# A recommendation kernel on one core: a ninth table looked up by matrix product in three of eight halves, gathers in groups of 4, 3, 4, 4, 3

## The chip, the cores and the metric

The kernel runs on one core of a Trainium2 chip. The metric is the device time of one execution in microseconds (us); lower is better. TensorE (PE) multiplies matrices, VectorE (DVE) and ScalarE (ACT) copy and compute, GpSimd (POOL) issues the gathers, SyncE (SP) issues most other DMA transfers. Each engine works through its own queue in order; they tell each other of progress by semaphores.

## The reference

```
e = stack([tbl_f[ids[:, f]] for f in range(26)], axis=1)     # (2048, 26, 128) fp32
combined = concatenate([e, dense_x[:, None, :]], axis=1)     # (2048, 27, 128)
interact = einsum('bfd,bgd->bfg', combined, combined)        # 27x27 dot products of each sample
z = interact[:, triu_i, triu_j]                              # the 351 pairs above the diagonal
h = concatenate([z, dense_x], axis=1)                        # (2048, 479)
h = relu(h @ W_top1 + b_top1)                                # 512
h = relu(h @ W_top2 + b_top2)                                # 256
y = h @ W_top3                                               # 1
```

There are 2048 samples and 26 embedding tables: eight of 1000 rows, nine of 1250, eight of 12500 and one of 125000.

## The kernel before, in words

The samples go through in 16 tiles of 128; two tiles make a half of 256 (h = t // 2), so there are 8 halves, an even and an odd tile each.

**Gathered tables.** 18 tables are fetched row by row: for each tile and table POOL issues one indirect DMA (L266) of 128 rows into one of 14 buffers of `rows`. PE turns each with a transpose (L283, `turn(t, n)`) into a bank of `ps_feat`, and ACT copies the bank into `feat` (L531). Gathers and turns go in five groups a tile, n = 0 to 4, of 4, 4, 4, 4 and 2 tables. Before a group POOL waits for `turned`, until the group that last used its buffers, 14 gathers earlier, was turned (`turns_before`, L93). For every tile this works out so: group 0 waits for group 1 of the tile before, group 1 for its group 2, group 2 for its group 3; groups 3 and 4 both wait for group 0 of their own tile.

**Kept tables.** The eight tables of 1000 rows lie in SBUF, each as 8 chunks of 125 rows, split into a high and a low part. They are looked up with products for a whole half, two tables at a time (`look_up(h, p)`, pairs p = 0 to 3). First PE spreads the ids of a pair over all partitions (L293, `spread_ids`) and ACT copies them to one of 3 buffers `ids_all` (L568). DVE compares them with row numbers and so builds one-hot columns (L766, `build`), in units of two chunks, in a ring of 10 units `hot`. PE multiplies each chunk twice (L319 high part, L321 low part), 32 matmuls a pair, and tells of each unit with `hot_free`. ACT copies the found rows (L544 for the even tile into `feat`, L547 for the odd one into `stage`, from where `unstage`, L574, moves them).

**Products and layers.** `products(t, b)`, b = 0 to 3, computes the dot products of a tile (L340, 16 matmul records each) into one of two banks `ps_gram`; ACT and DVE copy half each into `z` (L517, `take`). SP packs `z` into columns with nine small DMAs a tile (L205, `pack`). `split_half` (ACT, L586) and `rest_zp` (DVE, L752) split them, then come `layer1` and `layer2` (L349), `layer3` (L426).

**The order** of each engine is written out by hand for an even and an odd tile (`even(t)`, `odd(t)` on PE, ACT and DVE). The work that goes through the two `ps_feat` banks has one common numbering, `feat_turns` (L62); PE waits before using a bank until the use two places earlier was copied out (`bank_free`). On PE an even tile ends with `look_up(h, 3)`, `turn(t, 3)`, `layer2(h - 2, 0)`, `turn(t, 4)`, `layer2(h - 2, 1)`. The ids of the kept tables for the next half are loaded by SP (L214) and turned into numbers by ACT (L558, `number_ids`) into a second buffer.

## Time and profile before

| what | value |
|---|---|
| median of 3 runs | 522.01 us |
| lowest and highest | 517.69 and 525.85 us |
| the profiled execution | 515.37 us |
| its span, first to last instruction | 513.3 us |
| PE, DVE, ACT, POOL busy | 81, 48, 45, 55 % |
| mean granted TensorE clock | 0.900 |
| gathers | 288, mean 973 ns on POOL |

The span is what the profile covers; 2.07 us of the profiled execution lie around it. In a timeline each row is an instruction or a run of equal ones: start, duration, instruction with output and inputs and its count, and in brackets the idle time of that engine before it and who ended it. "issue" means that no wait was found; "remote" that the semaphore's update came at a time at which none of the instructions that send it had just ended. The ends of matmuls are modelled.

### The profile page before, as it was taken

The page shows a single profiled execution, that of the slowest core. Times are in us where ns is not written, and L with a number is a line of the kernel's source. Part 1 is how long each engine was busy: PE and PEld are TensorE (multiplying, and loading weights), DVE is VectorE, ACT ScalarE, POOL GpSimd, SP SyncE. Part 2 cuts the span into 40 slices and gives each one's busy share as a digit, 9 for nine tenths or more (in the row PEclk, how much of TensorE's full clock was granted, in tenths as well). Part 3 has the DMA queues.
Part 4 walks back from the last instruction along what each step waited for, and adds up shares of the span by engine and source line. Part 5 has one row for each costly group of instructions (what it writes and reads, how often), then busy time and mean ns, then how long its engine had stood idle before and what let it go on. Part 6 is the DMA issues. An engine that isn't in the chain of part 4 may idle for free.

```text
span 513.3 us, 8017 instructions
## 1 busy us (share of the span) xinstructions
PE 414.9 (81%) x2976; PEld 385.6 (75%) x2976; DVE 247.9 (48%) x715; ACT 232.7 (45%) x428; POOL 282.9 (55%) x297
## 2 busy tenths in 40 slices
PE   6697739586896979788797979889687877968887
PEld 4586638485895968787797859879687867967786
DVE  7383937434665245542564327533455426721332
ACT  3364516254453635434544435446354346334734
POOL 6666754656464663666546565466536575464210
PEclk9897959798897979999797988989798998997999
DMA  8921221122211121122211222121211222122100
GB/s 225 289 70 36 70 56 27 49 50 69 50 37 46 48 73 38 42 62 67 52 33 47 52 67 58 32 53 52 72 32 47 58 72 53 33 54 54 31 18 6
DMA packets 21488, 30.54 MB, mean 59 GB/s; under 512 B 6986, under 2 KB 15680, under 8 KB 21323
## 3 DMA queue, kind: packets, MB, share of 16 engines
q0 software_dynamic: 9312, 19.00, 14.3%
q1 hardware_dynamic: 11852, 10.83, 8.1%
q8 instruction: 24, 0.39, 0.3%
q10 hardware_dynamic: 287, 0.21, 0.2%
q14 instruction: 13, 0.11, 0.1%
HBM read 26.86 MB, written 0.01 MB: 52 GB/s over the span
## 4 chain that ended last, share of the span: by engine, by line
PE 46%; another core or an unknown queue 27%; ACT 19%; issue 7%; DMA 0%; ACTq 0%; DVE 0%
PE ps_gram L340 16%; PE ps_mlp L349 8%; PE ps_feat L319 7%; PE ps_feat L321 6%; ACT feat L531 5%; ACT z L517 3%; PE ps_feat L283 3%; ACT feat L574 3%; ACT feat L544 2%; PE ps_feat L316 2%; ACT ids_all L568 1%; PE ps_feat L293 1%; ACT stage L547 1%; PE ps_mlp L426 1%
## 5 line engine op out<-in xcount | busy, mean ns | idle before, releaser
L266 POOL DMA_INDIRECT rows<-in_tbl,ids_now x288 | 280.3, 973 | 197.5 <-PE ps_feat L283 76.1
L766 DVE TENSOR_SCALAR hot<-ids_all,row_no 125x256 fp32r<-125x256 f32 x512 | 159.0, 378 | 46.6 <-remote 21.2
L319 PE MATMUL ps_feat<-hot,table_hi 125*128 125x256 f32 x480 | 137.0, 316 | 17.6 <-issue 11.3
L321 PE MATMUL ps_feat<-hot,table_lo 125*128 125x256 f32 x480 | 135.0, 312 | 10.7 <-issue 10.6
L340 PE MATMUL ps_gram<-feat 128*123 128x108 f32 x1024 | 127.1, 281 | 3.8 <-ACT feat L531 3.7
L340 PEld LDWEIGHTS ps_gram<-feat 128*123 128x123 f32 x1024 | 121.9, 196 | 7.6 <-ACT feat L531 4.4
L517 DVE COPY z<-ps_gram 27x208 f32<-27x208 f32 x128 | 46.9, 367 | 156.6 <-PE ps_gram L340 87.0
L319 PEld LDWEIGHTS ps_feat<-hot,table_hi 125*128 125x128 f32 x480 | 105.0, 219 | 19.2 <-issue 10.3
L321 PEld LDWEIGHTS ps_feat<-hot,table_lo 125*128 125x128 f32 x480 | 104.9, 219 | 17.2 <-issue 16.9
L544 ACT COPY feat<-ps_feat 128x256 f32<-128x256 f32 x32 | 19.4, 607 | 143.7 <-remote 94.3
L517 ACT COPY z<-ps_gram 27x208 f32<-27x208 f32 x128 | 41.6, 325 | 94.9 <-remote 48.0
L531 ACT COPY feat<-ps_feat 128x512 f32<-128x512 f32 (+1 forms) x80 | 77.6, 976 | 10.7 <-remote 9.8
L283 PE MATMUL ps_feat<-ident,rows 128*128 128x128 f32 x288 | 46.5, 281 | 10.1 <-ACT stage L547 6.1
L293 PE MATMUL ps_feat<-ids_few_no,ident_r 128*128 128x512 f32 x32 | 17.8, 574 | 38.4 <-ACT stage L547 26.1
L283 PEld LDWEIGHTS ps_feat<-ident,rows 128*128 128x128 f32 x288 | 34.1, 146 | 13.4 <-issue 12.8
L293 PEld LDWEIGHTS ps_feat<-ids_few_no,ident_r 128*128 128x128 f32 x32 | 7.2, 228 | 42.7 <-ACT stage L547 19.0
L349 PE MATMUL ps_mlp<-zp_hi,w_hi 128*128 128x256 f32 x112 | 34.1, 304 | 1.9 <-ACT hid_lo_before L605 1.8
L349 PE MATMUL ps_mlp<-zp_lo,w_hi 128*128 128x256 f32 x112 | 32.7, 292 | 0.1
L349 PE MATMUL ps_mlp<-zp_hi,w_lo 128*128 128x256 f32 x112 | 32.5, 290 | 0.0
L752 DVE TENSOR_TENSOR hid_lo<-hid_lo_before,hid_hi 128x256 fp32r<-128x256 f32 x32 | 13.5, 422 | 26.8 <-ACT hid_hi L608 26.6
L349 PEld LDWEIGHTS ps_mlp<-zp_hi,w_hi 128*128 128x128 f32 x112 | 22.6, 202 | 2.4 <-ACT hid_lo_before L605 2.2
L349 PEld LDWEIGHTS ps_mlp<-zp_lo,w_hi 128*128 128x128 f32 x112 | 22.5, 201 | 0.6 <-issue 0.3
(73 smaller groups left out, 329.2 us busy)
## 6 DMA issues: line engine op xcount, KB each, us to landing
rows<-in_tbl,ids_now POOLq DMA_INDIRECT x288
table_lo_before<-in_tbl SPq DMA_DIRECT2D x8, 448.0 KB
dense<-in_dense_t SPq DMA_DIRECT2D x8, 128.0 KB
w_lo_before<-in_w SPq DMA_DIRECT2D x1, 1024.0 KB
zp_lo_before<-in_dense_t SPq DMA_DIRECT2D x8, 128.0 KB
zp_lo_before<-z SPq DMA_DIRECT2D x15, 39.0 KB
zp_lo_before<-z SPq DMA_DIRECT2D x15, 36.0 KB
w_lo_before<-in_w SPq DMA_DIRECT2D x1, 512.0 KB
```

The lines of the kernel that those rows point to most:

```text
L266: nc.gpsimd.indirect_dma_start(rows[:, row_at(t, f), :], None, gathered[f], bass.IndirectOffsetOnAxis(ap=ids_now[:, t, f:f + 1], axis=0),) ...
L283: mm = nc.tensor.transpose(ps_feat[at % 2][:, k * P:(k + 1) * P], rows[:, row_at(t, f), :], ident[:])
L293: nc.tensor.matmul(ps_feat[at % 2][:], ident_r[:, p:p + 1].broadcast_to([P, P]), ids_few_no[:].rearrange("p k s -> p (k s)"), start=True, ...
L319: nc.tensor.matmul(result, table_hi[:, CHUNK_AT[n] + ch, :], columns, start=first, stop=False)
L321: mm = nc.tensor.matmul(result, table_lo[:, CHUNK_AT[n] + ch, :], columns, start=False, stop=last)
L340: mm = nc.tensor.matmul(ps_gram[at % 2][0:FOUR, c, 0:4 * F], four[:, 0:FOUR], four.rearrange("d (j f) -> d j f", f=FPAD)[:, :, 0:F], start ...
L349: mm = nc.tensor.matmul(ps_mlp[at % 2][:, 0:HALF], w[:, c, n * P:(n + 1) * P], x[:, c, :], start=(c == 0 and k == 0), stop=(c == ZP_CHUNKS ...
L517: op = copy(z[q:q + F, :, 32 * j + BATCH * b:32 * j + BATCH * (b + 1)], ps_gram[at % 2][32 * j:32 * j + F, :, F * j + 1:F * (j + 1)].rearr ...
L531: copy(feature(t, group.start, group.stop), by_group(ps_feat[at % 2][:, 0:P * len(group)].rearrange("d (f s) -> d f s", s=P))).then_inc(em ...
L544: copy(feature(2 * h, GATHERED + first, GATHERED + stop), by_group(found[:, :, 0:P]))
L574: copy(feature(t, GATHERED, TABLES), by_group(stage[:])).then_inc(unstaged, 1)
L766: op = nc.vector.tensor_scalar(hot[0:VROWS, u % HOTS, c, :], ids[0:VROWS, k, :], row_no[0:VROWS, no + UNIT * i + c:no + UNIT * i + c + 1], ...
```

## The change

A ninth table, the first of 1250 rows (10 chunks of 125), is loaded into SBUF beside the eight. In halves 1, 2 and 4 (`LOOKED_UP_LAST`) it is looked up with products, as a fifth "pair" of one table (`LAST`); in the other five it is gathered, as before, as the last table of group 4. So a tile has 17 gathers in halves 1, 2 and 4 and 18 in the others, 282 in all for 288. The look-up stands on PE between `turn(t, 3)` and `layer2(h - 2, 0)` of the even tile; its ids are spread at the end of the odd tile before; DVE builds its one-hot columns before `take(t - 1, 3)`.

The groups are of 4, 3, 4, 4 and 3 tables (2 in the last one where the ninth is looked up). The buffers of `rows` go by a running count of gathers, and with them the waits: after a tile of 18 gathers group 0 of the next waits for group 2 (not 1) of the tile before; after one of 17 it waits for group 1, as it did. The waits of the other groups are as they were.

The numbers of the ids are written over the ids themselves (one buffer for the two, 32 partitions long), so SP loads the next half's ids only when all ids of this half are spread (before: once they were numbered). At the start the load of half 1's ids moves behind the weights, and the ninth table is loaded last; it is split on ACT and DVE behind the first odd tile. `y` has no buffer of its own: it is written over a row of `hid2`, and the wait for its transfer stands before the next `hid2` instead. The diff, cut:

```diff
@@ -23,22 +23,27 @@
 VROWS, SPRAYED = 125, 112
-CHUNKS = [8] * 8
+CHUNKS = [8] * 8 + [10]
 KEPT = len(CHUNKS)
+ALWAYS = KEPT - 1
+LOOKED_UP_LAST = (1, 2, 4)
 CHUNK_AT = [sum(CHUNKS[:n]) for n in range(KEPT + 1)]
 UNIT = 2
-UNITS = CHUNK_AT[KEPT] // UNIT
 HOTS = 10
 IDS = 3
-PAIRS = (KEPT + 1) // 2
-PAIR = [range(2 * p, min(2 * p + 2, KEPT)) for p in range(PAIRS)]
+
+IDS_ROWS = 32
+PAIRS = ALWAYS // 2
+LAST = PAIRS
+PAIR = [range(2 * p, min(2 * p + 2, KEPT)) for p in range(PAIRS + 1)]
 WHOLE_FIRST = 4
-SPLIT_AT = {n: i for i, n in enumerate([*range(WHOLE_FIRST, KEPT), *range(WHOLE_FIRST)])}
+SPLIT_AT = {n: i for i, n in enumerate([*range(WHOLE_FIRST, ALWAYS), *range(WHOLE_FIRST), ALWAYS])}
 SIZES = sorted(set(CHUNKS))
 ROW_NO_AT = {n: sum(SIZES[:i]) for i, n in enumerate(SIZES)}
-GATHERED = TABLES - KEPT
-GROUPS = [range(f, min(f + 4, GATHERED)) for f in range(0, GATHERED, 4)]
-TURNS = len(GROUPS)
+GATHERED = TABLES - ALWAYS
+GROUP_SIZES = (4, 3, 4, 4, 3)
+TURNS = len(GROUP_SIZES)
+GROUPS = [range(sum(GROUP_SIZES[:n]), sum(GROUP_SIZES[:n + 1])) for n in range(TURNS)]
 ROWS = 14
...
@@ -57,6 +62,20 @@
...
+def pairs_in(h):
+    return PAIRS + (h in LOOKED_UP_LAST)
+def group_of(t, n):
+    group = GROUPS[n]
+    return range(group.start, group.stop - (n == TURNS - 1 and t // 2 in LOOKED_UP_LAST))
+GATHERS = [(t, n, f) for t in range(TILES) for n in range(TURNS) for f in group_of(t, n)]
+GATHER_AT = {(t, f): i for i, (t, n, f) in enumerate(GATHERS)}
...
@@ -68,32 +87,42 @@
         h = t // 2
         if t % 2 == 0:
             order += [("tile", t, 0), ("pair", h, 2), ("tile", t, 1), ("ids", h + 1, 0), ("tile", t, 2),
-                      ("ids", h + 1, 1), ("pair", h, 3), ("tile", t, 3), ("tile", t, 4)]
+                      ("ids", h + 1, 1), ("pair", h, 3), ("tile", t, 3), ("pair", h, LAST), ("tile", t, 4)]
         elif h + 1 < HALVES:
             order += [("tile", t, 0), ("tile", t, 1), ("ids", h + 1, 2), ("tile", t, 2), ("pair", h + 1, 0),
-                      ("tile", t, 3), ("ids", h + 1, 3), ("pair", h + 1, 1), ("tile", t, 4)]
+                      ("tile", t, 3), ("ids", h + 1, 3), ("pair", h + 1, 1), ("tile", t, 4), ("ids", h + 1, LAST)]
         else:
             order += [("tile", t, n) for n in range(TURNS)]
-    return {x: n for n, x in enumerate(x for x in order if x[0] == "tile" or x[1] < HALVES)}
+    return {x: n for n, x in enumerate(x for x in order if x[0] == "tile" or x[1] < HALVES and x[2] < pairs_in(x[1]))}
 FEAT_AT = feat_turns()
+def ids_before(h):
+
+    return sum(pairs_in(i) for i in range(h))
+
+
 def units_before(h, n):
-    return UNITS * h + CHUNK_AT[n] // UNIT
+    return (sum(CHUNK_AT[PAIR[pairs_in(i) - 1].stop] for i in range(h)) + CHUNK_AT[n]) // UNIT
 def row_at(t, f):
-    return (GATHERED * t + f) % ROWS
+    return GATHER_AT[t, f] % ROWS
 def turns_before(t, f):
-    x = GATHERED * t + f - ROWS
-    return 0 if x < 0 else TURNS * (x // GATHERED) + x % GATHERED // 4 + 1
+    at = GATHER_AT[t, f] - ROWS
+    return 0 if at < 0 else TURNS * GATHERS[at][0] + GATHERS[at][1] + 1
+
+
+def landed(t, n):
+
+    return 16 * sum(len(group_of(i, n)) for i in range(t % 2, t + 1, 2))
 def bass_dlrm_tower(nc, dense_t, ids_gathered, ids_kept, gathered, kept, w1, b1, w2, b2, w3, out):
...
@@ -113,15 +142,16 @@
-        ident, ident_r = sb("ident", [P, P]), sb("ident_r", [P, PAIRS], F32R)
+        ident, ident_r = sb("ident", [P, P]), sb("ident_r", [P, PAIRS + 1], F32R)
         row_int, row_no = sb("row_int", [P, sum(SIZES)], I32), sb("row_no", [P, sum(SIZES)])
...
-        ids_few = sb("ids_few", [PAIRS, 2, HALF], I32)
-        ids_few_no = sb("ids_few_no", [P, 2, HALF], F32R)
+        at = (nc.sbuf_base + 31) // 32 * 32
+        ids_few_no = ctx.enter_context(nc.sbuf_tensor("ids_few_no", [P, 2, HALF], F32R, align_bytes=32))
+        ids_few = nc.alloc_sbuf_tensor_at("ids_few", [IDS_ROWS, 2, HALF], I32, offset=at)
         ids_all = sb("ids_all", [P, IDS, 2, HALF])
...
@@ -210,7 +245,7 @@
-                    sp.wait_ge(ids_few_ready, h)
+                    sp.wait_ge(ids_spread, ids_before(h))
                 sp.dma_start(ids_few[:], ids_kept[:, h * HALF:(h + 1) * HALF].rearrange("(p k) s -> p k s", k=2)
...
@@ -230,16 +265,17 @@
             load_ids(0)
-            for n in range(KEPT):
+            for n in range(ALWAYS):
                 load_table(sp, n)
             load_dense(0)
-            load_ids(1)
             sp.dma_start(w1_sb[:], w1).then_inc(weights_landed, 16)
...
             sp.dma_start(b2_sb[:], b2).then_inc(biases_landed, 16)
+            load_ids(1)
             load_dense(1)
+            load_table(sp, ALWAYS)
             for t in range(2, TILES + 2):
...
@@ -259,9 +295,10 @@
             for t in range(TILES):
-                for n, group in enumerate(GROUPS):
-                    if turns_before(t, group.stop - 1) > 0:
-                        pool.wait_ge(turned, turns_before(t, group.stop - 1))
+                for n in range(TURNS):
+                    group = group_of(t, n)
+                    if turns_before(t, group[-1]) > 0:
+                        pool.wait_ge(turned, turns_before(t, group[-1]))
                     for f in group:
...
@@ -441,6 +480,7 @@
                 turn(t, 3)
+                look_up(h, LAST)
                 layer2(h - 2, 0)
...
@@ -465,6 +505,7 @@
                 layer1(h - 1, 3)
+                spread_ids(h + 1, LAST)
...
@@ -527,51 +568,54 @@
...
-                if h > 0:
-                    act.wait_ge(ids_spread, PAIRS * h)
-                copy(ids_few_no[0:PAIRS, :, :], ids_few[:]).then_inc(ids_few_ready, 1)
+                copy(ids_few_no[0:IDS_ROWS, :, :], ids_few[:]).then_inc(ids_few_ready, 1)
...
@@ -716,6 +762,7 @@
             odd(1)
+            split_table(ALWAYS)
             act.wait_ge(weights_landed, 16 * 2)
...
@@ -799,6 +846,7 @@
                 put_dense(t)
+                build(h, LAST)
                 take(t - 1, 3)
```

The order of the gathers on POOL, from the last group of tile 0 on (in_tbl_N is the table, "waits turned" opens a group). Before:

```order
L266 DMA rows<-in_tbl_21,ids_now 128x128 [waits turned]
L266 DMA rows<-in_tbl_24,ids_now 128x128
L266 DMA rows<-in_tbl_0,ids_now 128x128 [waits turned]
L266 DMA rows<-in_tbl_1,ids_now 128x128
L266 DMA rows<-in_tbl_4,ids_now 128x128
L266 DMA rows<-in_tbl_5,ids_now 128x128
L266 DMA rows<-in_tbl_6,ids_now 128x128 [waits turned]
```

And after:

```order
L303 DMA rows<-in_tbl_21,ids_now 128x128 [waits turned]
L303 DMA rows<-in_tbl_24,ids_now 128x128
L303 DMA rows<-in_tbl_0,ids_now 128x128
L303 DMA rows<-in_tbl_1,ids_now 128x128 [waits turned]
L303 DMA rows<-in_tbl_4,ids_now 128x128
L303 DMA rows<-in_tbl_5,ids_now 128x128
L303 DMA rows<-in_tbl_6,ids_now 128x128
L303 DMA rows<-in_tbl_7,ids_now 128x128 [waits turned]
```

The last group has three gathers (21, 24 and 0, the ninth table), and the next tile begins one gather later.

DVE, from the last build of pair 3 in even tile 4 on (L766 and L813 build one-hot columns, L517 and L558 are takes, L775 and L822 put the dense feature). Before:

```order
L766 TENSOR_SCALAR hot<-ids_all,row_no 125x256 x16
L517 COPY z<-ps_gram 27x26x8 x2
L775 COPY feat<-dense 128x4x32
L517 COPY z<-ps_gram 27x26x8 x2
L766 TENSOR_SCALAR hot<-ids_all,row_no 125x256 x16
```

And after:

```order
L813 TENSOR_SCALAR hot<-ids_all,row_no 125x256 x16
L558 COPY z<-ps_gram 27x26x8 x2
L822 COPY feat<-dense 128x4x32
L813 TENSOR_SCALAR hot<-ids_all,row_no 125x256 x10
L558 COPY z<-ps_gram 27x26x8 x2
L813 TENSOR_SCALAR hot<-ids_all,row_no 125x256 x16
```

Ten comparisons stand ahead of the last take of the tile before.

PE, at the end of the same even tile: the last matmuls of pair 3, the turn of group 3, what follows. Before:

```order
L319 MATMUL ps_feat<-hot,table_hi 128x256
L321 MATMUL ps_feat<-hot,table_lo 128x256
L283 MATMUL ps_feat<-ident,rows 128x128 x4
L349 MATMUL ps_mlp<-hid_hi,w_hi 128x256
L349 MATMUL ps_mlp<-hid_lo,w_hi 128x256
```

And after:

```order
L358 MATMUL ps_feat<-hot,table_hi 128x256
L360 MATMUL ps_feat<-hot,table_lo 128x256
L320 MATMUL ps_feat<-ident,rows 128x128 x4
L358 MATMUL ps_feat<-hot,table_hi 128x256
L360 MATMUL ps_feat<-hot,table_lo 128x256
```

Behind the turn now stand 20 matmuls of the look-up, of which the first two are shown, and `layer2` comes after them.

## Rows read from the trace of the kernel before

**Rows 1.** The page: span, busy time by engine, chain that ended last.

```profile
span 513.3 us, 8017 instructions
PE 414.9 (81%) x2976; PEld 385.6 (75%) x2976; DVE 247.9 (48%) x715; ACT 232.7 (45%) x428; POOL 282.9 (55%) x297
PE 46%; another core or an unknown queue 27%; ACT 19%; issue 7%; DMA 0%; ACTq 0%; DVE 0%
```

**Rows 2.** Waits, longest first: engine, line waited for, us, times, longest us.

```profile
ACT feat L544 <- remote: 94.3, 18, 9.5
```

**Rows 3.** Timeline, POOL, tiles 9 to 11: start, us, instruction, idle before and releaser.

```profile
292.23 0.94 POOL L266 DMA_INDIRECT rows<-in_tbl,ids_now  x1 [1.17 <-PE ps_feat L283]
...
306.98 0.94 POOL L266 DMA_INDIRECT rows<-in_tbl,ids_now  x1 [2.46 <-remote]
...
324.46 0.94 POOL L266 DMA_INDIRECT rows<-in_tbl,ids_now  x1 [5.50 <-PE ps_feat L283]
...
333.36 0.94 POOL L266 DMA_INDIRECT rows<-in_tbl,ids_now  x1 [1.72 <-remote]
...
345.79 0.94 POOL L266 DMA_INDIRECT rows<-in_tbl,ids_now  x1 [2.64 <-remote]
```

**Rows 4.** Timeline, PE, the same stretch.

```profile
296.10 1.87 PE L340 MATMUL ps_gram<-feat 128*123 128x108 f32 x16
...
299.26 0.60 PE L283 MATMUL ps_feat<-ident,rows 128*128 128x128 f32 x4
...
321.80 1.95 PE L340 MATMUL ps_gram<-feat 128*123 128x108 f32 x16
...
325.67 0.36 PE L319 MATMUL ps_feat<-hot,table_hi 125*128 125x256 f32 x1
...
329.55 0.60 PE L283 MATMUL ps_feat<-ident,rows 128*128 128x128 f32 x4
...
334.94 0.63 PE L283 MATMUL ps_feat<-ident,rows 128*128 128x128 f32 x4 [0.45 <-ACT feat L531]
335.40 2.85 PE L340 MATMUL ps_gram<-feat 128*123 128x108 f32 x16
```

**Rows 5.** Timeline, ACT, the same stretch.

```profile
306.55 0.67 ACT L517 COPY z<-ps_gram 27x208 f32<-27x208 f32 x2 [6.54 <-remote]
...
323.79 0.66 ACT L517 COPY z<-ps_gram 27x208 f32<-27x208 f32 x2 [0.88 <-PE ps_gram L340]
...
333.07 0.59 ACT L544 COPY feat<-ps_feat 128x256 f32<-128x256 f32 x1 [5.83 <-remote]
...
338.29 0.66 ACT L517 COPY z<-ps_gram 27x208 f32<-27x208 f32 x2 [1.25 <-issue]
...
345.50 0.64 ACT L544 COPY feat<-ps_feat 128x256 f32<-128x256 f32 x1 [5.93 <-remote]
345.91 0.43 ACT L547 COPY stage<-ps_feat 128x256 f32<-128x256 f32 x1
```

**Rows 6.** Timeline, PE, end of even tile 10.

```profile
342.75 0.60 PE L283 MATMUL ps_feat<-ident,rows 128*128 128x128 f32 x4
...
346.49 0.41 PE L283 MATMUL ps_feat<-ident,rows 128*128 128x128 f32 x2
```

**Rows 7.** Groups by shape: busy us, mean ns of one, idle before.

```profile
L266 POOL DMA_INDIRECT rows<-in_tbl,ids_now x288 | 280.3, 973 | 197.5 <-PE ps_feat L283 76.1 <-issue 73.5 <-remote 46.1
L293 PE MATMUL ps_feat<-ids_few_no,ident_r 128*128 128x512 f32 x32 | 17.8, 574 | 38.4 <-ACT stage L547 26.1 <-ACT ids_all L568 4.9 <-ACT ids_few_no L558 3.9
L766 DVE TENSOR_SCALAR hot<-ids_all,row_no 125x256 fp32r<-125x256 f32 x512 | 159.0, 378 | 46.6 <-remote 21.2 <-PE ps_feat L321 14.9 <-PE ps_feat L316 5.2
L752 DVE TENSOR_TENSOR table_lo<-table_lo_before,table_hi 125x1024 fp32r<-125x1024 f32 x8 | 9.5, 1222 | 0.4 <-ACT table_hi L692 0.4
```

**Rows 8.** Timeline, SP's DMA issues, pack of tile 9.

```profile
339.11 7.42 SPq L205 DMA_DIRECT2D zp_lo_before<-z  x9
```

**Rows 9.** Timeline, ACT, tile 11.

```profile
354.74 1.05 ACT L586 CAST zp_hi<-zp_lo_before 128x1024 fp32r<-128x1024 f32 x1 [0.44 <-issue]
```

85 lines of the change are left out of this document (50 added, 35 removed).

## The prediction

> **What bounds the kernel now.** I read the page first. PE is the busiest engine, 414.9 of 513.3 us, yet it carries only 46 % of the chain that ended last; 27 % stands under "another core or an unknown queue" and 19 % under ACT [rows 1]. One core runs, so the 27 % must be waits whose release the profile can't place. The list of waits says where: ACT before L544 (it empties a looked-up pair) waited 94.3 us "remote", 18 times [rows 2]. So I went to the timelines of POOL, PE and ACT over tiles 9 to 11.
>
> The last product of tile 8 ends on PE at 296.10 + 1.87 = 297.97; ACT, which has nothing else to do, copies it at 306.55, after 6.54 us idle [rows 4, 5]. That is 8.6 us late. The product that ends at 321.80 + 1.95 = 323.75 is copied at 323.79, 0.04 us late [rows 4, 5]. What differs is POOL. Its gathers follow each other every 0.94 + 0.30 = 1.24 us. From 292.23 to 306.98 - 2.46 = 304.5 it issues ten in one run; in the 5.5 us before 324.46 it issues none [rows 3]. The same shows in the even tile: the look-up's last matmul ends just before 329.55, ACT sees it at 333.07, and POOL's run of six ends at 333.36 - 1.72 = 331.6 [rows 3 to 5]. Pair 3 is over before 342.75, ACT sees it at 345.50, POOL's run of eight ends at 345.79 - 2.64 = 343.15 [rows 3, 5, 6]. So an update by PE that falls late into a run of gathers is seen 1.4 to 2.4 us after the run's end. Early in a run it isn't late: the product that ends at 335.40 + 2.85 = 338.25, 4.9 us into a run, is copied at 338.29 [rows 3 to 5]. Rows never are late: the gathers that end at 292.23 - 1.17 = 291.06 are turned at 299.26 [rows 3, 4]. The half thus goes round a loop: run of gathers, PE's updates come through, `turned` lets POOL start the next run. Gathers cost time though PE never waits for a row.
>
> **The look-up's price on PE.** Pair 2 takes from 325.67 to 329.55, 3.88 us for 32 matmuls, 0.121 each [rows 4]. Twenty more are 2.42 us. Two transposes go (about 0.1 us each), and an ids matmul of 256 columns comes: half of 574 ns, 0.29 [rows 7]. Net 2.5 us in each of three halves, **+7.5**. All of it is on the chain, since PE is what runs there between two waits.
>
> **Its place.** The look-up needs the bank of pair 3, which ACT frees at 345.91 + 0.43 = 346.34 [rows 5]. Before, PE filled the time from 342.75 to 346.49 with a `layer2` and turned group 4 at 346.49 [rows 6]. Now it reaches the look-up first, stands until 346.34, and `layer2` (12 matmuls, 1.45 us) comes after it and has lost its cover. That happens in halves 2 and 4; half 1 has no `layer2` there yet. **+2.9.**
>
> **The split of the ninth table**: DVE 1.222 x 1.25 = 1.53 us [rows 7], and the cast on ACT ahead of it, for which I take as much, once, between tiles 1 and 2; other work of PE covers them partly: 0 to 3, I take **+1**.
>
> **Gathers saved.** Six, each 1.24 us of a run [rows 3]. In the even tile of halves 1, 2 and 4 the second run has seven for eight; in the odd tile the run behind the ten has three for four. Where updates wait for the run's end, each saved gather brings PE forward by 1.24: six are -7.5; if the lateness isn't the gathers' doing, 0. The rows speak for the first: **-7.5**.
>
> At this place a rule of the Trainium skill speaks against my reading. "SBUF — State Buffer", section "SBUF: two separate sides", says that DMA ports and engine ports are disjoint, that a DMA can't be slowed by compute nor the reverse, and that PE never waits on anyone there. By it the saved gathers would bring nothing. The trace doesn't show which port is busy; it shows the lateness next to the runs. The second rival below gives the time for that.
>
> **The groups.** In halves 1, 2, 4 the runs keep their shape (6, 7, 4 and 10, 3, 4). In halves 3, 5, 6, 7 group 0 waits for group 2 of the tile before, so an even tile has runs of 7, 7, 4 (before 6, 8, 4) and an odd one 7, 7, 4 (before 10, 4, 4). Even tile: the first run ends 1.24 later. The second started at 333.36 with group 1's turn; now it starts with group 2's, which ends at 334.94 + 0.63 = 335.57 [rows 3, 4], pushed by the same 1.24: 336.8 and 0.3 to start, 3.8 later. With one gather less it ends 2.6 later. If the look-up of pair 3 is caught by it, +2.6; but it now falls earlier into the run, where updates came through, and then pair 3 is seen at once, 1.2 earlier than at 345.50. Between +2.6 and -1.2, near the middle: +0.7, four times. Odd tile: the run of ten, behind which the product was 8.6 us late, becomes seven, 3.7 us shorter; the next is seven for four and gives back all of it or nothing: 0 to -4, I take -2, three times. Together 4 x 0.7 - 3 x 2 = **-3** (bounds -17 and +10.6).
>
> **Costed at nothing.** DVE's ten comparisons (378 ns each, 3.8 us [rows 7]) stand before the last take, and the later of them wait for pair 3's first units; the take, now at about 338.3 as ACT's [rows 5], may slip to where pair 3's updates come through, 345.5. PE needs it for the product after next. SP's `pack`, nine DMAs in 7.42 us from 339.11 [rows 8], then starts near 346 and ends at 353.6, and ACT splits at 354.74 [rows 9]: the cover of 8.2 us shrinks to 1 and what the landing takes may stick out; but the half is up to 4 us longer there too. If it fails it costs some 2 us, three times. The load of ids now waits for the last spread, in a half with the ninth table just before the product at 321.80 [rows 4]; the numbering waits for it, and what is queued behind the numbering on ACT, L544, comes only at 333.07 [rows 5]: 11 us of cover. The pack of the tile before, behind that load on SP, slips too, but is needed only at 354.74 [rows 9]. `y` in `hid2` is sent well before `hid2` is written again.
>
> **The sum.** 7.5 + 2.9 + 1 - 7.5 - 3 = +0.9 on the profiled execution's 515.37 us (513.3 us of it span). The median of the runs is 522.01, 6.6 above it, and I add to that: **523 us**.
>
> **The rivals.**
> *Shorter runs break the lateness.* If the 8.6 us come from a run's length and not from the sum of gathers, the odd tiles of halves 3, 5, 6 gain 4 each (-12), the even ones 1.2 each four times (-4.8), and the saved gathers 7.5: 11.4 - 7.5 - 12 - 4.8 = -13, 509 us. For it: six gathers made 3.4 us of lateness (329.7 to 333.07), ten 8.6 [rows 4, 5], more than in proportion. Against it: the second run follows at once, and the total of gathers in such a half stays 36.
> *The lateness is PE's own.* Runs may end late because `turned` comes late, not the reverse. Then neither shape nor number of gathers counts, and 7.5 + 2.9 + 1 = +11.4 remain: 533 us. By the rule that the Trainium skill's "SBUF — State Buffer", section "SBUF: two separate sides", states, it would come out so. Against it: PE is as busy before 323.75, without gathers, and on time.
> *The second run catches the look-up.* Slower: in the four even tiles the longer and later run holds pair 3, +2.6 each (10.6), the odd tiles gain nothing, and half of the saved gathers lie where PE would have waited anyway (-3.7): 11.4 + 10.6 - 3.7 = +18, 540 us. It decides from the point where the units of pair 3 fall more than some 5 us into the run; before, an update 4.9 us into one was on time [rows 3 to 5].
> *The ninth table isn't worth its place at all*, the ids late: ACT would stand before L558; 11 us of cover make this the least likely, +3 a half, 532.
>
> **How the numbers follow.** Forecast 0.48 (515 to 531), shorter runs 0.20, PE's own 0.17, second run 0.12, ids 0.03. The range for 8 in 10 reaches to most of the faster case and up to the slower one: 505 to 539. A measurement of this kernel tells 2 %, 10.4 us, from no change: faster is below 511.6, slower above 532.4. Faster: two thirds of 0.20 and a tail of the forecast, 0.18. Slower: half of 0.20, the 0.12 and a tail, 0.26. The rest, 0.56, is no change.
>
> **What would show it.** Right, if in tile 11's like the product before the run of seven is seen within 2.5 us of the run's end; if PE stands before the look-up of the ninth table until ACT's L547 counterpart ends; if tiles of halves 1, 2 and 4 are longer than their neighbours by 0 to 4 us. The gather term is wrong if a half with 34 gathers has as much "remote" waiting as one with 36. The forecast falls if the odd tiles of halves 3, 5, 6 shrink by more than 4 us, or if the even ones grow by more than 3; or if ACT waits before its split of `zp`.

## The result, and the profile after

The kernel after takes 540.72 us (median of 4 runs, 537.57 to 545.97) beside 521.36 us of the kernel before (4 runs, 517.69 to 525.85): ratio 1.0376, interval 1.0285 to 1.0466. It is slower; 523 with a range up to 539 and 0.26 for slower had been forecast. The profiled execution took 545.97 us, its span is 544.2 us, 30.9 more than before [rows 1]. Ratios and intervals here leave out executions over 1.5 % above the fastest of the same kernel, and this profiled one is such. The medians differ by 19.4 us and the two profiled executions by 30.6, so some 11 us of what the two traces differ by is spread between executions. What only this pair of traces shows is known to a few us at best.

The page of the kernel after: span, busy times, the chain that ended last, and the group of the gathers (count, busy us, mean ns, idle before and what ended most of it).

```profile
span 544.2 us, 8172 instructions
PE 425.6 (78%) x3033; PEld 396.7 (73%) x3033; DVE 256.2 (47%) x747; ACT 234.9 (43%) x438; POOL 280.9 (52%) x292
PE 50%; another core or an unknown queue 25%; ACT 15%; issue 7%; POOL 1%; DMA 1%; DVE 0%; ACTq 0%
L303 POOL DMA_INDIRECT rows<-in_tbl,ids_now x282 | 278.3, 987 | 226.8 <-PE ps_feat L320 108.4
```

Its list of waits: engine, line waited for, us in total, times, longest us.

```profile
ACT feat L585 <- remote: 114.7, 16, 14.3
POOL rows L303 <- PE ps_feat L320: 108.4, 25, 7.8
```

PE has 10.7 us more work, yet a smaller share (78 % for 81 %): the other 20 us are idle time of PE. The waits grew: ACT before it empties a looked-up pair, 94.3 to 114.7 us [rows 2]; POOL before a group of gathers for PE's turn, 76.1 to 108.4 us though there are six gathers fewer [rows 7]. The first of the two says little by itself: in two traces of the kernel after with its old groups (below) it is 87.9 and 121.2 us. POOL's is 77.4 and 84.6 us there. L303, L320, L358 and L360, L379, L558, L572, L585, L588, L799, L813 are what L266, L283, L319 and L321, L340, L517, L531, L544, L547, L752, L766 were.

Where the 30.9 us lie is told by the starts of each tile's first product in the timelines of PE, as differences from one tile to the next ("rows of" names the tile that PE turns and looks up in that stretch):

| stretch, product of tile | rows of tile | before | after | difference | group 0 behind it waits later |
|---|---|---|---|---|---|
| to 0 | 0 | 45.55 | 42.40 | -3.1 | yes |
| 0 to 1 | 1 | 34.38 | 42.94 | +8.6 | yes |
| 1 to 2 | 2, ninth looked up | 27.50 | 34.54 | +7.0 | no |
| 2 to 3 | 3 | 33.47 | 32.43 | -1.0 | no |
| 3 to 4 | 4, ninth looked up | 28.71 | 30.82 | +2.1 | no |
| 4 to 5 | 5 | 32.73 | 30.33 | -2.4 | no |
| 5 to 6 | 6 | 26.49 | 28.97 | +2.5 | yes |
| 6 to 7 | 7 | 33.15 | 33.47 | +0.3 | yes |
| 7 to 8 | 8, ninth looked up | 26.66 | 31.14 | +4.5 | no |
| 8 to 9 | 9 | 33.16 | 30.68 | -2.5 | no |
| 9 to 10 | 10 | 26.38 | 30.94 | +4.6 | yes |
| 10 to 11 | 11 | 33.11 | 33.26 | +0.1 | yes |
| 11 to 12 | 12 | 26.33 | 31.47 | +5.1 | yes |
| 12 to 13 | 13 | 33.07 | 33.07 | 0 | yes |
| 13 to 14 | 14 | 28.29 | 27.92 | -0.4 | yes |
| 14 to the end of the span | 15 | 44.29 | 49.78 | +5.5 | |

Half of the loss stands in the stretches from product 0 to 2, whose waits no step of the prediction had looked at.

The same differences to the kernel before, in us, from the traces of experiments on other slower chips (they are explained below) tell which rows belong to the later wait of group 0:

| stretch | later wait in all tiles, nothing else moved (two chips) | new groups alone | kernel after with the old groups (two chips) |
|---|---|---|---|
| 0 to 1 | +9.3, +9.4 | +9.5 | +0.2, -0.5 |
| 1 to 2 | -0.1, +3.9 | +0.2 | +3.3, +3.8 |
| 9 to 10 | +4.4, +4.1 | +3.1 | +2.0, +0.7 |
| 11 to 12 | +4.0, +4.2 | +3.3 | -0.1, +1.6 |
| 14 to the end | +2.4, +1.5 | +5.8 | +3.0, +4.3 |

So the +8.6 at the start and most of the +4.6 and +5.1 of even tiles come with the later wait. The +7.0 is in part the ninth look-up, and the end grows without the wait too.

**An even tile without the ninth look-up (12).** Timelines of the kernel after; POOL, then PE, then ACT.

```profile
404.59 0.94 POOL L303 DMA_INDIRECT rows<-in_tbl,ids_now  x1 [7.78 <-PE ps_feat L320]
...
417.75 0.94 POOL L303 DMA_INDIRECT rows<-in_tbl,ids_now  x1 [4.71 <-PE ps_feat L320]
...
429.51 0.94 POOL L303 DMA_INDIRECT rows<-in_tbl,ids_now  x1 [3.21 <-remote]
```

```profile
401.92 0.79 PE L379 MATMUL ps_gram<-feat 128*123 128x108 f32 x5
...
416.39 1.08 PE L320 MATMUL ps_feat<-ident,rows 128*128 128x128 f32 x4 [0.24 <-ACT feat L572]
...
424.21 0.60 PE L320 MATMUL ps_feat<-ident,rows 128*128 128x128 f32 x4
...
428.06 0.28 PE L388 MATMUL ps_mlp<-hid_hi,w_hi 128*128 128x256 f32 x1 [2.10 <-issue]
...
430.18 0.87 PE L320 MATMUL ps_feat<-ident,rows 128*128 128x128 f32 x3 [0.82 <-ACT stage L588]
...
433.39 0.79 PE L379 MATMUL ps_gram<-feat 128*123 128x108 f32 x6
```

```profile
414.73 0.59 ACT L585 COPY feat<-ps_feat 128x256 f32<-128x256 f32 x1 [7.36 <-remote]
...
429.22 0.60 ACT L585 COPY feat<-ps_feat 128x256 f32<-128x256 f32 x1 [7.60 <-remote]
429.61 0.42 ACT L588 COPY stage<-ps_feat 128x256 f32<-128x256 f32 x1
```

Counted from the tile's first product (401.92 here, 321.80 in [rows 4], a tile of the same kind; the times before are those of [rows 3, 5]): the first run, of seven, ends at 417.75 - 4.71 = 413.04 and ACT sees pair 2 at +12.8 (before +11.3, 333.07). The second run starts at +15.8 for +11.6, since it now waits for group 2's turn at 416.39. It too has seven and ends at 426.30. PE is through with pair 3 before 424.21, but ACT sees it at 429.22, +27.3 for +23.7: 2.9 us after the run's end. In the other even tiles with this wait, 6, 10 and 14, pair 3 is seen after the run's end too, 2.3, 3.2 and 0.8 us later in the tile than before. Then a second loss, of PE's clock. Windows of the same kernel: stretch, its length, busy us of PE, PEld, DVE, ACT, POOL with counts, granted clock, DMA share, GB/s.

```profile
425.70:430.10 4.40, 0.94 (x5) 0.62 (x4) 1.12 (x5) 0.88 (x3) 1.19 (x2) 0.98 0.26 61
430.20:433.40 3.20, 3.20 (x16) 3.20 (x17) 0.63 (x2) 1.77 (x3) 2.29 (x4) 0.51 0.17 44
433.40:440.00 6.60, 6.60 (x57) 5.79 (x57) 1.46 (x4) 3.99 (x8) 3.92 (x5) 1.00 0.17 42
```

PE is nearly idle for 4.4 us, and group 4's turn and `layer2` behind that run at a granted 0.51, the 1.2 GHz level: 3.2 us where the kernel before took 1.7, from 346.49 [rows 6] to its next product at 348.18. Its product, and the window ahead of it:

```profile
348.18 1.08 PE L340 MATMUL ps_gram<-feat 128*123 128x108 f32 x8
```

```profile
346.50:348.20 1.70, 1.70 (x15) 1.68 (x15) 1.13 (x4) 1.60 (x3) 1.18 (x2) 1.00 0.30 74
```

So pair 3 is seen 3.6 us later in tile 12, and the clock adds 1.5: 5.1 us. In tile 10 the granted clock is 0.52 in the 3.5 us before the product; in tiles 6 and 14 it is 1.00 there.

PE itself stands too. At 428.06 it takes up the next matmul of `layer2` after 2.10 us in which no wait is found ("issue"), 1.8 us behind the run's end. In every trace from a slower chip there are such stands of 0.4 us and more, 6 to 41 of them (29.9 us in all in the kernel before, 26.0 in the kernel after), and in the eleven traces from faster chips there is none. So what is late here may be PE and not only the news of it; no run tells the two apart.

**The ninth look-up** does stand before ACT's copy of pair 3, as forecast: 0.46 us in tile 2, 3.03 in tile 4, 0.91 in tile 8. The longest:

```profile
176.06 0.39 PE L358 MATMUL ps_feat<-hot,table_hi 125*128 125x256 f32 x1 [3.03 <-ACT stage L588]
```

**The start.** Timelines of the kernel after, POOL and DVE, the last matmul of the pair, and ACT's longest wait; ahead of them the same gather in the kernel before.

```profile
30.92 1.34 POOL L266 DMA_INDIRECT rows<-in_tbl,ids_now  x1 [2.89 <-PE ps_feat L283]
```

```profile
35.32 5.48 POOL L303 DMA_INDIRECT rows<-in_tbl,ids_now  x1 [7.28 <-PE ps_feat L320]
...
76.44 1.02 POOL L303 DMA_INDIRECT rows<-in_tbl,ids_now  x1 [3.23 <-remote]
```

```profile
33.68 4.03 DVE L813 TENSOR_SCALAR hot<-ids_all,row_no 125x256 fp32r<-125x256 f32 x15
37.63 2.35 DVE L799 TENSOR_TENSOR table_lo<-table_lo_before,table_hi 125x1024 fp32r<-125x1024 f32 x2
```

```profile
62.31 0.28 PE L360 MATMUL ps_feat<-hot,table_lo 125*128 125x256 f32 x1
```

```profile
76.15 0.60 ACT L585 COPY feat<-ps_feat 128x256 f32<-128x256 f32 x1 [14.33 <-remote]
```

Group 0 of tile 1 begins at 35.32 after 7.28 us of waiting (before: 30.92 after 2.89), and its first gather takes 5.48 us for 1.34. With that it ends 8.5 us later (40.80 for 32.26), and product 1 comes at 85.34 for 79.93, 5.4 us later and +8.6 behind a product 0 that came 3.1 sooner. In the three other traces from slower chips with the later wait this gather ends 6.2, 10.7 and 10.7 us later than in the kernel before, and product 1 comes 3.9, 7.8 and 7.9 later: all but 2 to 3 us of the delay is passed on. The next 24 follow without a pause, to 73.22: 25 in one run, where the kernel before had runs of 8, 4 and 14. PE's last matmul of the pair started at 62.31 (62.59 with its modelled end); ACT sees it at 76.15 after 14.33 us idle.

### The profile page after: what moved, and what is told of

It reads as the page before. It is cut to its first block, busy times and chain, and to the rows that moved or that the text cites. A ratio compares the mean times of both kernels' runs of the same rounds, so it can differ in the third digit from the quotient of the medians.

```text
span 544.2 us, 8172 instructions
## 1 busy us (share of the span) xinstructions
PE 425.6 (78%) x3033; PEld 396.7 (73%) x3033; DVE 256.2 (47%) x747; ACT 234.9 (43%) x438; POOL 280.9 (52%) x292
## 4 chain that ended last, share of the span: by engine, by line
PE 50%; another core or an unknown queue 25%; ACT 15%; issue 7%; POOL 1%; DMA 1%; DVE 0%; ACTq 0%
PE ps_gram L379 18%; PE ps_mlp L388 8%; PE ps_feat L360 8%; PE ps_feat L358 8%; ACT feat L572 5%; PE ps_feat L320 3%; ACT z L558 2%; ACT feat L585 2%; PE ps_feat L355 2%; ACT feat L618 2%; PE ps_mlp L465 1%; ACT ids_all L609 1%; POOL rows L303 1%; ACT stage L588 1%
## 5 line engine op out<-in xcount | busy, mean ns | idle before, releaser
L303 POOL DMA_INDIRECT rows<-in_tbl,ids_now x282 | 278.3, 987 | 226.8 <-PE ps_feat L320 108.4
L813 DVE TENSOR_SCALAR hot<-ids_all,row_no 125x256 fp32r<-125x256 f32 x542 | 166.3, 373 | 78.6 <-remote 40.3
L358 PE MATMUL ps_feat<-hot,table_hi 125*128 125x256 f32 x510 | 139.8, 308 | 21.0 <-ACT feat L572 9.5
L379 PE MATMUL ps_gram<-feat 128*123 128x108 f32 x1024 | 135.0, 289 | 15.9 <-ACT feat L572 9.3
L379 PEld LDWEIGHTS ps_gram<-feat 128*123 128x123 f32 x1024 | 128.7, 205 | 22.1 <-ACT feat L572 10.9
L360 PE MATMUL ps_feat<-hot,table_lo 125*128 125x256 f32 x510 | 137.1, 302 | 5.6 <-issue 5.6
L358 PEld LDWEIGHTS ps_feat<-hot,table_hi 125*128 125x128 f32 x510 | 107.2, 210 | 24.4 <-ACT feat L572 11.2
L558 DVE COPY z<-ps_gram 27x208 f32<-27x208 f32 x128 | 46.9, 366 | 147.0 <-PE ps_gram L379 84.4
L360 PEld LDWEIGHTS ps_feat<-hot,table_lo 125*128 125x128 f32 x510 | 107.2, 210 | 7.7 <-issue 7.4
L585 ACT COPY feat<-ps_feat 128x256 f32<-128x256 f32 (+1 forms) x35 | 20.8, 593 | 163.9 <-remote 114.7
L558 ACT COPY z<-ps_gram 27x208 f32<-27x208 f32 x128 | 41.6, 325 | 88.8 <-PE ps_gram L379 45.7
L572 ACT COPY feat<-ps_feat 128x512 f32<-128x512 f32 (+2 forms) x80 | 75.9, 954 | 8.0 <-remote 5.3
L320 PE MATMUL ps_feat<-ident,rows 128*128 128x128 f32 x282 | 47.7, 288 | 25.3 <-ACT stage L588 11.6
L320 PEld LDWEIGHTS ps_feat<-ident,rows 128*128 128x128 f32 x282 | 34.5, 149 | 30.0 <-issue 24.9
L331 PE MATMUL ps_feat<-ids_few_no,ident_r 128*128 128x512 f32 (+1 forms) x35 | 18.7, 547 | 37.1 <-ACT stage L588 29.1
L799 DVE TENSOR_TENSOR hid_lo<-hid_lo_before,hid_hi 128x256 fp32r<-128x256 f32 x32 | 13.5, 423 | 30.1 <-ACT hid_hi L652 29.9
```

The lines of the kernel that those rows point to most:

```text
L303: nc.gpsimd.indirect_dma_start(rows[:, row_at(t, f), :], None, gathered[f], bass.IndirectOffsetOnAxis(ap=ids_now[:, t, f:f + 1], axis=0),) ...
L320: mm = nc.tensor.transpose(ps_feat[at % 2][:, k * P:(k + 1) * P], rows[:, row_at(t, f), :], ident[:])
L331: nc.tensor.matmul(ps_feat[at % 2][:, 0:HALF * n], ident_r[:, p:p + 1].broadcast_to([P, P]), ids_few_no[:, 0:n, :].rearrange("p k s -> p ( ...
L358: nc.tensor.matmul(result, table_hi[:, CHUNK_AT[n] + ch, :], columns, start=first, stop=False)
L360: mm = nc.tensor.matmul(result, table_lo[:, CHUNK_AT[n] + ch, :], columns, start=False, stop=last)
L379: mm = nc.tensor.matmul(ps_gram[at % 2][0:FOUR, c, 0:4 * F], four[:, 0:FOUR], four.rearrange("d (j f) -> d j f", f=FPAD)[:, :, 0:F], start ...
```

## Experiments

The kernel before takes 515.7 to 524.1 us on some chips and 403.5 to 404.0 us on others; I call them the slower and the faster chips. Each chip was used at one time only, so whether it is the chip itself or something set at the time isn't told apart. Each ratio is to the kernel before on the same chip at the same time. Some expectations are for a slower chip alone; where the run fell on a faster one, they stand untested.

### Slower chip, kernel before 515.7 us (7 runs)

**The groups alone**, in the kernel before.

```diff
-GROUPS = [range(f, min(f + 4, GATHERED)) for f in range(0, GATHERED, 4)]
+GROUP_SIZES = (4, 3, 4, 4, 3)
+GROUPS = [range(sum(GROUP_SIZES[:n]), sum(GROUP_SIZES[:n + 1])) for n in range(TURNS)]
```

> The kernel before with the groups 4, 3, 4, 4, 3 alone: no ninth table, ids numbered into their own buffer. Theory A (the groups make group 0 wait for a later turn, and PE and POOL lose about 4 to 5 us a half by it, more at the start): 535 to 545 us, halves of some 64.5 us for 59.5. Theory B (the cost lies in the ninth table, its load and the ids in place): within 1 % of before.

Measured: 550.66 us, 1.0665 (1.0571 to 1.0758), above the range of theory A, which has the right cause.

**The kernel after with the old groups.**

```diff
-GROUP_SIZES = (4, 3, 4, 4, 3)
+GROUP_SIZES = (4, 4, 4, 4, 2)
```

> The changed kernel with the groups put back to 4, 4, 4, 4, 2; the ninth table and the ids in place stay. Theory A: 520 to 528 us, about the kernel before, since halves 1, 2 and 4 of the changed kernel are only 0 to 2 us longer than before. Theory B: 535 us or more, the start as slow as in the changed kernel.

Measured: 524.17 us, 1.0187 (1.0123 to 1.0252), within theory A's range.

**One wait moved**: the kernel before with its own groups, but group 0 waits one turn later.

```diff
-                        pool.wait_ge(turned, turns_before(t, group.stop - 1))
+                        pool.wait_ge(turned, turns_before(t, group.stop - 1) + (n == 0))
```

> The kernel before with its own groups, but group 0 of each tile waits for group 2 of the tile before instead of group 1. Nothing else moves. If the later wait is the cause (theory A in its narrow form): 533 to 543 us, with a gap of 4 to 5 us before the second run of gathers in even tiles. If it is the run's length or the group of three that costs, this stays within 1 % of before.

Measured: 551.36 us, 1.0706 (1.0631 to 1.0780), more than forecast. Its waits:

```profile
ACT feat L544 <- remote: 163.3, 20, 10.0
...
POOL rows L266 <- PE ps_feat L283: 107.0, 29, 9.0
```

The same 35 us as the new groups cost, with the old sizes: the later wait alone costs as much as the new groups, and nothing is left over that the sizes would have to explain. Both waits grew, as in the kernel after. Here the later wait stands in all tiles, in the kernel after in nine of fifteen. Repeated on a second slower chip (kernel before 524.12 us):

> The kernel before with nothing changed but that group 0 waits one turn later (1.0706 where the kernel before takes 516 us). Theory: where the kernel before takes 403 us, it costs the start alone: a wait of 2 to 3 us before the gather number 18, 5.5 us for this gather in place of 1.3, and the row that comes late by it, in all 8 to 14 us, ratio 1.02 to 1.035, with halves of 45 to 46 us after. Rival (updates of PE are seen at once there, so a wait one turn later costs nothing, and the start of the kernel after is the third table's or the look-up's): 0.997 to 1.005. Where the kernel before takes 516 us: 1.06 to 1.08 again.

Measured: 558.16 us, 1.0664 (1.0582 to 1.0745).

**No gathers in tiles 8 to 11**: the kernel before without those 72 gathers (these tiles use stale rows).

```diff
+                if t in NO_GATHERS:      # range(8, 12)
+                    continue
```

> The kernel before without the gathers of tiles 8 to 11 (left out: those tiles use rows of earlier tiles, so their results are other ones). If PE's updates are late because gathers run: halves 4 and 5 fall from 59.5 us to 46 to 50 each, with no lateness over 0.1 us there, and the time falls by 20 to 27 us. If the lateness is PE's own: halves 4 and 5 stay at 58 us or more.

Measured: 479.42 us (one run), 36 less than 515.7 where 20 to 27 were expected. One window of this kernel in that stretch, and one of the kernel before over the like tiles:

```profile
229.00:317.00 88.00, 87.42 (x740) 84.71 (x739) 52.73 (x174) 55.89 (x104) 5.95 (x7) 1.00 0.09 22
```

```profile
289.00:408.00 119.00, 100.87 (x746) 94.62 (x746) 57.94 (x174) 55.56 (x104) 68.80 (x73) 0.91 0.20 52
```

The same work of four tiles takes 88 us with PE busy throughout at full clock, and 119 us beside gathers: PE stands 18 us, and is busy for 13 us more at a lower mean clock (0.91). ACT's late updates at the looked-up pairs, 27.6 us in the second window, are gone from the list of the first. PE waited for no row. So 72 gathers cost 31 us inside this window and 36 over the whole run, 0.5 us each. The gathers' transfers and POOL's waits for PE are gone with them; which of the three costs the time this run doesn't tell.

### Faster chip, kernel before 403.46 us (25 runs)

**A ring of 18**: the kernel before with `ROWS = 18` for 14, so each group waits for its own turn of the tile before. That is one turn earlier for each group, and two for group 3.

> The kernel before with 18 buffers for gathered rows instead of 14, so that group n of a tile waits for group n of the tile before: every wait of POOL is an earlier one. If the loop of POOL's waits sets the pace (theory A turned round: an earlier wait gains what the later one cost): 490 to 508 us, halves of 55 to 58 us. If long runs of gathers make PE's updates late by their length: runs of 14 and more appear and the time rises, 522 to 545 us. No difference: the wait of group 0 alone matters, in one direction.

Measured: 403.52 us, 0.9989 (0.9958 to 1.002). On another faster chip (403.69 us) it was 403.12 us, 0.9980 (0.9946 to 1.0014).

**No look-up**: the kernel after with old groups and `LOOKED_UP_LAST = ()`, so that the ninth table is loaded and split but always gathered.

> The changed kernel with the old groups 4, 4, 4, 4, 2 and no look-up of the ninth table (288 gathers; its load and split, the order of the loads and the ids in place stay). If the 8 us that the version with old groups lost come from the load, the split and the ids in place: 522 to 527 us, as with the look-ups. If they come from the look-ups: within 2 us of the kernel before.

Measured: 404.61 us, 1.0012 (0.9985 to 1.0039).

**In place only**: the same without loading and splitting the ninth table.

> As the one without look-ups, and without the ninth table's load and split: what is left of the change is the ids numbered in place, their later load, its place behind the weights, and y in hid2. If these cost nothing, as forecast: within 2 us of the kernel before. If the load of ids is late or SP's pack slips onto the path: 3 us or more above it.

Measured: 403.22 us, 0.9992 (0.9961 to 1.0023). Ids numbered in place, their later load and `y` in `hid2` cost nothing there, as forecast. The load and split cost at most 1.4 us, which is within the intervals.

**Six gathers fewer**: the kernel before without the last gather in tiles 2 to 5, 8 and 9 (its turn uses stale rows).

```diff
+                        if f == GATHERED - 1 and t // 2 in FEWER:      # (1, 2, 4)
+                            continue
```

> The kernel before with six gathers fewer, the last of group 4 in tiles 2 to 5, 8 and 9 (left out: their turns use stale rows), and no look-up. The forecast's term: -7.5 us, 1.24 each. By the kernel without the gathers of four tiles (72 gathers, 36 us) it should be 0.5 each: -3 us. If PE's updates weren't the gathers' doing: 0.

Measured: 398.11 us, 0.9860 (0.9813 to 0.9907): by the ratio 5.6 us, 0.94 a gather.

### Faster chip, kernel before 403.69 us (31 runs)

**Both kernels again.**

> The kernel before itself, for its trace on this chip. Ratio 1.00 within 1%. What it shows: the busy time of a half's gathers (36 of them at 0.94 us each), whether they stand back to back, and how long after its turn PE's update is seen. Where the kernel takes about 403 us the waits of the gathers for PE should be under 20 us in all (76.1 us in the trace of the 513.3 us span); where it takes 516 us they should be 70 to 85 us.

> The kernel after once more, unchanged, since one call's kernel before took 516 us and another's 403 us. Theory (the price is that of the later wait of group 0 under late updates of PE): where the kernel before takes 516 to 522 us, the ratio is 1.03 to 1.045 and starts to starts of 18-gather halves are 63.5 to 66 us. Where the kernel before takes about 403 us, no update is late, the wait of group 0 costs nothing and only the six saved gathers are left: ratio 0.985 to 0.995, some 397 to 401 us. Rival (the change costs by its own instructions: groups, look-up, split): slower on either, by 2% or more.

Measured: before 404.18 us (0.9998); after 406.84 us, 1.0054 (1.0017 to 1.0092), not the gain that I expected. The pages of the two, the kernel before first: span, chain, gathers.

```profile
span 402.3 us, 8017 instructions
...
POOL 54%; PE 24%; issue 17%; DMA 4%; ACT 0%; DVE 0%
...
L266 POOL DMA_INDIRECT rows<-in_tbl,ids_now x288 | 283.3, 984 | 89.3 <-issue 86.2
```

```profile
span 408.1 us, 8172 instructions
...
PE 58%; POOL 27%; issue 8%; ACT 3%; DMA 3%; DVE 0%; ACTq 0%
...
L303 POOL DMA_INDIRECT rows<-in_tbl,ids_now x282 | 284.2, 1008 | 92.8 <-issue 83.8
```

Here nothing is "remote" on the chain: gathers stand back to back and set the pace, 36 of them 45.0 us a half, and a half of the kernel before takes 45.0 to 46.2 us between products 3 and 13. Its list of waits has POOL waiting for PE for 1.2 us in all. After two tiles the kernel after is 13.5 us behind (93.54 for 80.01); over the rest of the span it wins back 7.7, and six gathers at 1.25 are 7.5. Its start on POOL and DVE:

```profile
30.09 5.48 POOL L303 DMA_INDIRECT rows<-in_tbl,ids_now  x1 [2.55 <-PE ps_feat L320]
...
45.81 5.86 POOL L303 DMA_INDIRECT rows<-in_tbl,ids_now  x1 [0.30 <-issue]
```

```profile
32.41 2.35 DVE L799 TENSOR_TENSOR table_lo<-table_lo_before,table_hi 125x1024 fp32r<-125x1024 f32 x2
...
45.45 4.27 DVE L813 TENSOR_SCALAR hot<-ids_all,row_no 125x256 fp32r<-125x256 f32 x16
49.65 1.21 DVE L799 TENSOR_TENSOR table_lo<-table_lo_before,table_hi 125x1024 fp32r<-125x1024 f32 x1
```

and what PE waited for:

```profile
59.20 1.11 PE L320 MATMUL ps_feat<-ident,rows 128*128 128x128 f32 x4 [10.23 <-DMA rows<-in_tbl,ids_now]
```

The first of the two long gathers ends at 35.57, 0.81 after DVE's operation; the second at 51.67, 0.81 after DVE's operation ended at 50.86. Each begins in the middle of a string of comparisons that runs into L799 without a gap. The wait (2.55 for the usual 0.30) and the excess over 0.94 of the two gathers (4.5 + 4.9) are 11.7 us. But the kernel before has long gathers in its start too: over the first 40 gathers the excess is 5.1 us there and 12.5 here. So some 9.7 of the 13.5 us come from the wait and the long gathers. The rest isn't traced; 1.1 of it stands in the kernel after with the old groups as well (below). This execution took 409.98 us, 3 more than the median.

**The new groups with a ring of 18**, which removes the later wait and keeps the sizes.

> The kernel before with groups of 4, 3, 4, 4, 3 (550.66 us on the first chip, ratio 1.067) and a ring of 18 buffers in place of 14, so that each group waits for its own turn of the tile before, which for group 0 is two turns earlier than in the groups-only kernel. Theory (the later wait of group 0 is the price of the groups): where the kernel before takes 516 us or more, this one falls back to 0.98 to 1.02 of it. Rival (the sizes 3 and 4 themselves, not the wait): 1.05 or more as before. Where the kernel before takes about 403 us both expect 1.00, within 0.5%.

Measured: 403.35 us, 0.9978 (0.9946 to 1.001). On a second faster chip (403.99 us) 0.9982 (0.9964 to 1.0001), and on a third (403.8 us) 0.9986 (0.9951 to 1.0022):

> The kernel before with groups of 4, 3, 4, 4, 3 and a ring of 18, so that each group waits for its own turn of the tile before. Where the kernel before takes 516 to 524 us, theory (the wait, not the sizes): 0.97 to 1.00, beside 0.9803 for the ring of 18 with the old groups and 1.0665 for these groups with the ring of 14. Rival (the sizes themselves cost): 1.04 or more. Where it takes 403 us: 0.9978 again within 0.5%.

> The kernel before with groups of 4, 3, 4, 4, 3 and a ring of 18, the third time, for a chip where the kernel before takes 516 to 524 us. There, theory (the wait, not the sizes): 0.97 to 1.00, beside 0.9803 for the ring of 18 with the old groups and 1.0665 for these groups with the ring of 14. Rival (the sizes themselves cost): 1.04 or more. Where the kernel before takes 403 us: 0.998 a third time, which tells nothing new.

All three fell on faster chips. Whether the sizes cost anything by themselves on a slower chip is therefore known only through the moved wait.

**The kernel after with the old groups**, on the faster chip where the kernel before takes 403.99 us.

> The kernel after with groups of 4, 4, 4, 4, 2, the third time. Where the kernel before takes 516 to 524 us it gave 1.0187 and 0.9964: 0.995 to 1.02 again. Where the kernel before takes 403 us, theory (gathers back to back set the pace; the start of the kernel after is lost by the wait of group 0 alone): six gathers of 1.25 us less, ratio 0.982 to 0.990. Rival (the look-ups cost by themselves): 0.997 to 1.005.

Measured: 398.98 us, 0.9885 (0.9819 to 0.9951), in span 396.7 us. The ninth table alone gains 5.0 us there, most of what six gathers are worth. The first gather of tile 1 comes without a wait, at 27.39, and takes 0.94 us; after two tiles the kernel stands at 81.11, where the kernel before stood at 80.01 on the chip above. With the new groups the same kernel is 1.0054 on a faster chip: it is they that turned this gain into a loss.

### Slower chip again, kernel before 524.12 us (13 runs)

> The kernel after with groups of 4, 4, 4, 4, 2 again (1.0187 where the kernel before takes 516 us). Theory (on a chip where the kernel before takes 403 us, gathers back to back set the pace and each costs 1.25 us, and all that the kernel after loses there is the start, 13.8 us over the first two tiles by the later wait of group 0): the six gathers saved are left, ratio 0.982 to 0.990, some 396 to 399 us. Rival (the look-ups themselves cost there, since the kernel after took 1.0054 in spite of the six gathers saved): 0.997 to 1.005. Where the kernel before takes 516 us: 1.01 to 1.025 again.

Measured: ten executions of 518.63 to 534.80 us with a median of 525.58; ratio 0.9964 (0.9912 to 1.0016). By the median of all ten it would be 1.003. The expectation, 1.01 to 1.025 again, wasn't met. With 1.0187 on the other slower chip the ninth table with the old groups costs between nothing and 2 % there.

> The kernel before with a ring of 18 buffers, so that groups 0 to 3 wait one turn earlier. Where the kernel before takes 403 us: 1.00 within 0.5%, as measured there twice (0.9989, 0.998). Where it takes 516 us, theory: 0.94 to 0.99, since a wait one turn later cost 7% there. Rival (longer unbroken runs of gathers hold PE's updates back longer): 1.00 to 1.05.

Measured: 512.64 us, 0.9803 (0.9736 to 0.9870): faster, clear of no change though not clear of 2 %, on the one slower chip where it ran. It is the one edit that beats both kernels there, and it costs nothing on the faster ones (0.9989 and 0.9980). One turn later for group 0 costs 35 us; one turn earlier for every group, and two for group 3, gains 11. Its waits:

```profile
ACT feat L544 <- remote: 91.8, 15, 17.9
...
POOL rows L266 <- PE ps_feat L283: 68.5, 30, 5.9
```

Against the trace of the kernel before, ACT's late updates are as many us [rows 2], POOL's waits 7.6 us fewer [rows 7]. The 17.9 us stand at its start, where 18 gathers now run at once: its first product comes at 54.03 for 45.55, and it wins 14.9 us from there on. The ring of 18 and the ninth table weren't tried together.

## Why the prediction was wrong

**The bound.** Right for the slower chips: gathers cost time in the kernel before though its rows are never late (36 us for 72 gathers). What it couldn't know from one trace is that this isn't so on all chips; on others the same kernel is bound by POOL.

**The step that failed: the groups, -3.** It had the longer run catch pair 3 only half of the time, odd tiles gain 2 us each, and the start at nothing. The runs showed a cost instead: pair 3 is caught in all four even tiles (+11.8 for +2.8), odd tiles gain nothing (+0.5 for -6), and the first tiles lose 8.6 us and more.
*Its even tile, +0.7.* The start of the second run was right (3.8 later forecast, 4.3 measured), and so was the first run's end. But I took pair 3 as seen somewhere between caught (+2.6) and at once (-1.2). It was caught in all four tiles, 2.3, 3.2, 3.6 and 0.8 us later than before, 2.5 in the mean, so the upper bound was the right price. Ahead of the product of tiles 10 and 12 the clock had fallen besides, +1.5 in tile 12, for which I had no term; in tile 14 it was at 0.50 in the kernel before already and at 1.00 in the kernel after, which gives some back. Measured +2.5, +4.6, +5.1 and -0.4: +11.8 for +2.8.
*Its odd tile, -2.* Measured +0.3, +0.1 and 0. The shorter first run does end the lateness sooner: ACT sees the product 1.3 us behind its end (446.11 after 444.81 in the timelines), as forecast. Nothing of it is left at the end of the tile; that the second run gives it back is the likely reading and isn't shown. With the later wait in all tiles odd stretches even grow, by 0.1 to 3.1 us in three traces.
*Half 0 left out.* I named halves 3, 5, 6 and 7 as those with the later wait and forgot tiles 1 and 2, which also follow tiles of 18 gathers. There it cost most, +15.6 with half 1's look-up in it, of which the look-up's part is 3.3 to 3.8 by the traces with the old groups. All kept tables are split on DVE at that time, and a delayed gather meets them. The end, +5.5, is the wait only in part: the wait alone gives +1.5 and +2.4 there, and the kernel after with the old groups grows by 3.0 and 4.3; what else costs there stays open. These two are 21 of the 30.9 us.

**The look-up, +7.5, its place, +2.9, and the gathers saved, -7.5.** For a half with `layer2` there the terms give 2.5 + 1.45 - 1.24 = +2.7 in the even tile and -1.24 in the odd one, +1.5 together. Measured: half 2 +2.1 and -2.4, half 4 +4.5 and -2.5, so -0.3 and +2.0. Right in sign in all four, and near in sum, half 2 partly by luck: the rows were read in tiles 9 to 11, and the runs don't keep their shape where I said so. Tile 4 of the kernel before has runs of 10, 4, 4, with both pairs seen at once, and tile 4 of the kernel after 6, 7, 4. For the whole kernel with the old groups the terms leave 0.9 + 3 = +3.9 us, 0.8 %; measured 1.9 % and -0.4 % on two slower chips. On the faster chip the six gathers alone gave 5.6 of the 7.5; on a slower chip they weren't tried alone, and 72 gathers gave 0.5 us each there for the 1.24 of the sum.

**The rule of the two sides.** The rival that I had put beside the Trainium skill's "SBUF — State Buffer", section "SBUF: two separate sides", was at 533 us. On the faster chips the section's sentence on DMA and engines agrees with the traces: no update of PE is late beside gathers. On the slower ones 72 gathers less are 36 us less, which it doesn't explain. The same section of the Trainium skill also says that DVE and GpSimd share a port pair that one of them locks for a whole instruction, among others when a DVE operation has two SBUF inputs and the GpSimd operation reads SBUF. That I had read past. A gather reads its ids from SBUF, and the long gathers agree with it: 5.48 and 5.86 us, each ending 0.8 us after L799. That a string of comparisons ahead of L799 lengthens them is seen in the traces and not explained by it.

**The rivals.** "The second run catches the look-up" (540 us, 0.12) was right in mechanism and in the price of the groups (10.6 for 11.8 measured), its odd tiles too. That its sum hits 540.72 is partly luck: the start was in no case, and it counted only half of the saved gathers. Shorter runs didn't break the lateness (0.20); PE's own lateness (0.17) falls with the run without gathers.

**Costed at nothing.** In place, `y` and the load of ids: 0.9992 on the faster chip. The first product came 3.1 us sooner, which I hadn't seen. It isn't the earlier weights: with them and the old groups it stands at 45.51 and 46.01 us, as before, and with the new groups alone it came 5.6 us sooner. There the first run of gathers is of 11 for 12.

**The profiled execution.** 523 was 0.9 on 515.37 plus 6.6 to the median; the difference to the median held (521.36 for four runs).

Still open: why PE's updates are seen late beside gathers on some chips and not on others, whether PE itself is held there, and what else costs at the end.

## To carry to other kernels

When buffers are regrouped, list for each group which turn it now waits for, for every tile from the first on. A wait one turn later cost 7 % on two slower chips with no other edit; on one of them waits one or two turns earlier gained 2 %. The start is a case of its own: there a delayed gather meets one-off work on other engines. And where a forecast rests on whether something is caught by a run or not, both outcomes are forecasts and their middle is none. Before a term is read from two traces, the spread between executions of the same kernel belongs beside it.
